# Head sums as two one-pass products of a rounded part and its remainder, and a new order of the recurrent layers' pieces

## The reference

```python
def step(s, rkvw):
    r_t, k_t, v_t, w_t = rkvw
    a = k_t[..., :, None] * v_t[..., None, :]
    out = jnp.einsum('bhi,bhij->bhj', r_t, u * a + s)
    s = a + w_t[..., :, None] * s
    return (s, out)
_, out = jax.lax.scan(step, s0, rkvw)
```

## Time and profile before

| | us |
|---|---|
| median of 3 runs (3200.41 to 3202.28) | 3200.64 |
| the profiled execution's own time | 3201.94 |
| its span (first to last instruction) | 3200.2 |
| busy: TensorE / VectorE / ScalarE | 3063.3 / 2338.7 / 1808.8 |
| recurrent steps end, attention starts, about | 2300 |

### The profile page before, as it was taken

The page is one execution under the profiler, slowest core; times in us unless marked ns, Lnnn a source line. Parts: engine busy times, 40 slices in busy tenths (PEclk is TensorE's granted clock), DMA queues, the critical chain, the costliest instruction groups (busy, mean ns, idle before and its releaser), DMA issues.

```text
span 3200.2 us, 77104 instructions
## 1 busy us (share of the span) xinstructions
PE 3063.3 (96%) x32684; PEld 2287.3 (71%) x32684; DVE 2338.7 (73%) x3819; ACT 1808.8 (57%) x3311; POOL 226.9 (7%) x457
## 2 busy tenths in 40 slices
PE   6899999999999999999999999997998998998998
PEld 4667777777777777777777777775665665665666
DVE  3788788887888787887887788876377566566566
ACT  3556555565655555555556555555366556556555
POOL 0000000000000000000000000000110101111010
PEclk8889999999999999999999999998999999999999
DMA  3223333343333333344333333343334224234131
GB/s 132 65 89 126 126 107 127 108 153 132 126 126 126 126 105 129 108 148 137 126 119 133 122 104 129 107 174 116 106 80 108 56 66 108 65 84 104 41 80 41
DMA packets 110357, 349.41 MB, mean 109 GB/s; under 512 B 22848, under 2 KB 56256, under 8 KB 84032
## 3 DMA queue, kind: packets, MB, share of 16 engines
q0 software_dynamic: 39936, 234.91, 23.2%
q1 hardware_dynamic: 69648, 106.28, 10.5%
q10 hardware_dynamic: 432, 3.28, 0.3%
HBM read 252.11 MB, written 16.78 MB: 84 GB/s over the span
## 4 chain that ended last, share of the span: by engine, by line
PE 87%; DVE 7%; ACT 4%; issue 1%; DMA 1%; SPq 0%; ACTq 0%; DVEq 0%
PE psum L734 42%; PE psum L743 6%; PE psum L901 5%; PE psum L919 4%; PE psum L871 3%; PE psum L800 3%; PE psum L861 3%; PE psum L784 3%; PE psum L891 3%; DVE psum L1727 2%; PE psum L876 2%; PE psum L687 2%; PE psum L699 2%; PE psum L867 1%; PE psum L667 1%; DVE mem L1732 1%
## 5 line engine op out<-in xcount | busy, mean ns | idle before, releaser
L734 PE MATMUL psum<-rw 128*128 128x256 f32 x6144 | 1402.8, 384 | 9.0 <-DVE rw L1529 5.4
L734 PEld LDWEIGHTS psum<-rw 128*128 128x128 f32 x6144 | 1155.1, 191 | 218.9 <-issue 54.0
L1727 DVE CUSTOM_DVE_ANT_0 psum<-psum,mem 128x1024 f32<-128x1024 f32 x256 | 313.6, 1225 | 77.3 <-PE psum L891 77.2
L1271 ACT ACTIVATE rest<-psum,mem 128x1024 f32<-128x1024 f32 x256 | 285.1, 1114 | 89.5 <-DVE mem L1727 87.8
L1523 DVE SCALAR_TENSOR_TENSOR rw<-psum,rw 128x256 f32<-128x256 f32 x480 | 196.0, 475 | 144.8 <-PE psum L700 79.5
L1183 ACT ACTIVATE rw<-psum,own 128x256 f32<-128x256 f32 x384 | 214.5, 714 | 123.7 <-PE psum L784 123.5
L901 PE MATMUL psum<-ident,rest 128*128 128x128 f32 x2048 | 270.4, 275 | 2.7 <-DVE mem L1686 1.6
L1624 DVE TENSOR_TENSOR_SCAN rw<-rw 128x2112 f32<-128x2112 f32 x48 | 217.4, 4529 | 70.6 <-ACT rw L1176 69.1
L901 PEld LDWEIGHTS psum<-ident,rest 128*128 128x128 f32 x2048 | 235.2, 141 | 42.3 <-issue 14.7
L1919 POOL DMA_DIRECT2D rw<-big_dram x192 | 101.7, 531 | 2157.2 <-PE psum L734 2124.3
L1264 ACT ACTIVATE mem<-psum 128x512 f32<-128x512 f32 x256 | 152.1, 595 | 141.0 <-PE psum L901 141.0
(11 more groups left out here) (157 smaller groups left out, 4297.4 us busy)
## 6 DMA issues: line engine op xcount, KB each, us to landing
rw<-big_dram POOLq DMA_DIRECT2D x192, 1024.0 KB, 5.6
side<-mem POOLq DMA_DIRECT2D x256, 128.0 KB, 4.1
rw<-xs_dram SPq DMA_DIRECT2D x32, 512.0 KB, 3.8
side<-mem SPq DMA_DIRECT2D x256, 64.0 KB, 2.0
rw<-rw SPq DMA_DIRECT2D x192, 64.0 KB, 2.0
rw<-rw SPq DMA_DIRECT2D x384, 32.0 KB
xs_dram<-rw SPq DMA_DIRECT2D x24, 512.0 KB, 6.4
rw<-x_dram SPq DMA_DIRECT2D x16, 512.0 KB, 5.0
```

What stands on the lines that cost most here:

```text
L734: last = mm(t[:, o * TC:(o + 1) * TC], big[:, k, P * m:P * m + P], src[:, k, 0:TC], start=k == 0, stop=k == KT - 1, skip_group_check=True)
L1271: s_ring.empty(f(probs[:, n % HPT, :].rearrange("p (a s) -> p a s", a=2), s_ring.bank(n, "s"), ACT.Exp, scale=-1.0, bias=mx[:, n % 8:n % 8 ...
L1727: maxima.inc(nc.vector.tensor_tensor_reduce(t, t, mbias.rearrange("p (a s) -> p a s", a=2), 1.0, 3.4e38, ALU.add, ALU.min, accum_out=mx[:, ...
```

## The change

Each factor tile is parted in two. ScalarE writes it rounded to float32r (`rounded`), VectorE writes factor minus rounded, again as float32r (`remainder`), and TensorE adds two float32r products with a float32r copy of `blk` in one PSUM tile. That is one more ScalarE and one more VectorE instruction for each of the nine tiles of a unit. The two parts have two buffers each (`high`, `low`), taken in turn: a rounding waits until TensorE is done with the tile two before. The factors themselves now lie in the mixtures' slots (`factors`). `blk` lies where `own_t0` is later, `add4` is dropped for `pick4`.

```diff
-    def sum_heads(it, name, src):
-        t = opened(b_ring, it, name)
-        b_ring.fill(mm(t, blk, src, start=True, stop=True), it, name)
...
+    def products(it, name):
+        if (it, name) == (0, "P0a"):
+            pe.wait_ge(blk_rounded, 1)
+        pe.wait_ge(low_dve.sem, low_dve.at(it, name))
+        n = SUMS.index(name) % 2
         t = opened(b_ring, it, name)
+        mm(t, blk_r[:].bitcast(F32R), high[n].bitcast(F32R), start=True, stop=False)
+        b_ring.fill(mm(t, blk_r[:].bitcast(F32R), low[n].bitcast(F32R), start=False, stop=True), it, name)
...
+    def rounded(it, name):
+        act.wait_ge(leaf.sem, leaf.at(it, name.lower()))
+        n = SUMS.index(name)
+        if n >= 2:
+            act.wait_ge(b_ring.full, b_ring.full_at(it, SUMS[n - 2]))
+        elif it:
+            act.wait_ge(b_ring.full, b_ring.full_at(it - 1, SUMS[-1]))
+        high_act.inc(f(high[n % 2].bitcast(F32R), factors(it, name), ACT.Copy), it, name)
...
+    def remainder(it, name):
+        dve.wait_ge(high_act.sem, high_act.at(it, name))
+        n = SUMS.index(name)
+        low_dve.inc(tt(low[n % 2].bitcast(F32R), factors(it, name), high[n % 2].bitcast(F32R).bitcast(F32), ALU.subtract), it, name)
...
-B_TILES = P0a P0b P1 P2a P2b VT0 VT1 KT0 KT1 P4a P4b P4c P4d U00 ...
+B_TILES = P0a P0b P1 P2a VT0 VT1 P2b P4a P4b KT0 KT1 P4c P4d U00 ...
-C_TILES = fr0 fr1 fk0 wo0 wo1 fk1 s1 fv0 fv1 m1 s2 i1
+C_TILES = fr0 fr1 fk0 wo0 fk1 wo1 fv0 s1 fv1 m1 s2 i1
```

More of the change, by code:

```diff
@@ L111 @@
 O_TILES = [("O0", "dve"), ("O1", "dve")]
-C_TILES = [(2, "fr0", "act"), (2, "fr1", "act"), (2, "fk0", "act"), (1, "wo0", "dve"), (1, "wo1", "dve"), (2, "fk1", "act"), (1, "s1", "act"), (2, "fv0", "dve"), (2, "fv1", "dve"), (1, "m1", "dve"), (1, "s2", "act"), (1, "i1", "dve")]
+C_TILES = [(2, "fr0", "act"), (2, "fr1", "act"), (2, "fk0", "act"), (1, "wo0", "dve"), (2, "fk1", "act"), (1, "wo1", "dve"), (2, "fv0", "dve"), (1, "s1", "act"), (2, "fv1", "dve"), (1, "m1", "dve"), (1, "s2", "act"), (1, "i1", "dve")]
@@ L124 @@
 F_ACT = ["kk0", "kk1"]
-CONSTS = 12
+SUMS = ["P0a", "P0b", "P1", "P2a", "P2b", "P4a", "P4b", "P4c", "P4d"]
+HIGH_ACT = list(SUMS)
+LOW_DVE = list(SUMS)
+CONSTS = 11
 def laid_out():
     at, n = {}, 0
-    for name, size in [("blk", P), ("pick4", P), ("pars", LAYERS * PARS), ("s_first", KT * B * 32), ("s_now", KT * B * 32),
+    for name, size in [("blk_r", P), ("pick4", P), ("pars", LAYERS * PARS), ("s_first", KT * B * 32), ("s_now", KT * B * 32),
                        ("first_edges", 2 * KT * B), ("half_edges", 2 * 2 * KT * B), ("small_w", SMALL)] + [(f"slot{i}", SLOT) for i in range(NSLOT)] + [
@@ L261, in build @@
         with nc.sbuf_tensor("rw", [P, RW_COLS], F32) as rw:
+            pass
+        parts_at, parts_size = RW_AT["parts"]
+        with nc.sbuf_tensor("blk_r", [P, P], F32) as blk_r, nc.sbuf_tensor("pick4", [P, P], F32) as pick4, \
+                nc.sbuf_tensor("between", [P, parts_at - 2 * P], F32), \
+                nc.sbuf_tensor("parts", [P, parts_size], F32) as parts:
             pass
@@ L843, in batch_tile @@
                     pe.wait_ge(*d_ring.empty_at(b, f"sum{sh}"))
-                    last = mm(t, add4[:], sums(b)[:, 512 * sh:512 * sh + 512], start=True, stop=True)
+                    last = mm(t, pick4, sums(b)[:, 512 * sh:512 * sh + 512], start=True, stop=True)
                 elif name[:4] == "mean":
@@ L946, in _ @@
                     products(b, "P2a")
-                    products(b, "P2b")
-                if 0 < n and has_n:
-                    norm_a(n, "i1")
+                if s == ITS:
+                    batch_tile(0, "k01")
                 if has_c:
@@ L953, in _ @@
                     values_by_token(b)
+                    products(b, "P2b")
+                if 0 < n and has_n:
+                    norm_a(n, "i1")
+                if has_e:
+                    feed(e, "fk", 1)
+                if has_b:
+                    products(b, "P4a")
+                    products(b, "P4b")
                 if has_c:
@@ L1765, in _ @@
                 if has_e:
-                    norm_c(e, "mixk")
+                    norm_c(e, "mixr")
+                if has_b:
+                    products1(b)
+                    level1(b)
                 if has_c:
+                    gated(c, 0)
                     gated(c, 1)
                 if has_b:
-                    level1(b)
+                    remainder(b, "P0a")
+                    remainder(b, "P0b")
+                if has_e:
+                    norm_c(e, "mixk")
+                if has_b:
+                    products2(b, 0)
+                    products2(b, 1)
+                    level2(b)
+                    own_values(b)
                 if 0 < n and has_n:
@@ L1789, in _ @@
                 if has_b:
-                    level4(b)
+                    remainder(b, "P4a")
+                    remainder(b, "P4b")
+                if s == ITS:
+                    after(0, "k00")
+                if has_c:
+                    residual(c, 0)
+                if has_b:
+                    gather(b, "P2b", "o2b", 0, 2)
+                if s == ITS:
+                    after(0, "k01")
+                if has_b:
+                    values(b, "P4a", 1, 4, 0)
                 if 0 < n and has_n:
@@ L1845, in _ @@
                 if has_b:
-                    scan(b, 1)
-                    own_turned(b, 1)
+                    group_mean(b, 0)
                 if has_n:
-                    mixed(n, "r")
+                    mixed(n, "g")
                 if has_c:
```

335 lines of the change are left out of this document (167 added, 168 removed).

## The result

| | before | after |
|---|---|---|
| median of 5 runs | 3200.72 us (3200.41 to 3202.28) | 3219.74 us (3212.38 to 3229.21) |
| profiled execution, its span | 3201.94, 3200.2 us | 3215.64, 3213.9 us |
| granted clock | 0.986 | 0.975 |
| first scan to first scan, mean of 21 steps | 90.08 us | 90.55 us |

The ratio is 1.0058 (95% interval 1.0037 to 1.0078). The forecast was 3123 us with a range of 3104 to 3162 and a chance of 0.04 for slower: it was wrong by 97 us and in its sign.

The account below looks back on a forecast made before the run. It took TensorE's list to bound the recurrent steps: 3.81 + 0.34 - 0.3 (handoffs) - 0.3 (DMA) = 3.55 us a step, times 22 is 78 us, from 3201.94, less 1.3 to the median: 3123 us, range 3104 to 3162.

Parts of the forecast that it names:

- which makes TensorE's list 90.03 - 4.15 = 85.9 us: TensorE's work in one steady step, summed from durations, falls by 4.15 us to 85.9 us.
- Products, 4.54 us: A step's nine head sums on TensorE, as float32r product pairs, take 4.54 us instead of 8.35, saving 3.81.
- Rival 4: Float32r products of the head sums run at the float32 pace, so nothing is saved there: 3206 us, chance 0.04.
- its 0.34 us go as well: TensorE's wait ahead of P4a for ScalarE to empty a bank disappears, since P4a moves ahead of the keys' transposes: 0.34 us.
- VectorE's chain, 86.2 us: The circle through VectorE's longest stretch and TensorE's list keeps a step from being shorter than 86.2 us, handoffs included.
- rival 1: VectorE's chain becomes the bound, its short operations holding the engine longer: step 87.7 us, 3150 us, chance 0.19.
- 0.3 for all handoffs: Small waits between TensorE's list and VectorE's chain cost 0.3 us a step, between 0 and 1.5.
- DMA, 0.3 us a step: The third group of updates waits 0.3 us a step for the copies of v_m, bounds 0 and 2.8.
- rival 2: The copies of v_m land late, a wait of 2.3 us a step instead of 0.3: 3167 us, chance 0.10.
- The turn of the buffers: Rounding waits for TensorE's tile two before, remainder for rounding, TensorE for remainder: some 1.6 us a turn.
- rival 3: The turn of the two buffers shows on TensorE and costs 4.7 us a step, slower than before: 3213 us, chance 0.05.
- 22 steps, nothing in the first and last: The saving counts in 22 TensorE-bound steps; the first and last unit's steps gain 0 each, bounds -3 and +4 us.

Follow-up runs that it names:

- a_r0: The changed kernel with r's first half projection back between the two halves of the state's outputs on TensorE; 3172.27 us, ratio 0.9914.
- c7: The changed kernel with s2 between k's halves, r's first half ahead of i1, third updates later, the second norm's reciprocal earlier on VectorE; 3147.37 us, 0.9834.
- the two pairs of kernels: The changed kernel and c7, each against its own order with single float32 products: 3219.7 against 3295.0 us, 3147.37 against 3222.89 us.
- a_wide: The changed kernel with neighbouring 32-column output products joined into 64 columns, half as many matmuls, outputs left wrong; 3129.21 us, 0.9778.
- a_plain: The changed kernel's order alone, each head sum one float32 product again, without roundings and subtractions; 3295.01 us, ratio 1.0301.

## Why the prediction was wrong, point by point

- **"which makes TensorE's list 90.03 - 4.15 = 85.9 us"**, taken as the time that TensorE needs for a step, is the step that failed. The list was summed from durations, as if TensorE had every instruction when it wants it; the sum put the supply of instructions and the clock behind a stall at nothing. Measured are 90.55 us a step, with 2.1 us of issue waits in the outputs alone (43.8 us in 24 times). The change joined four pieces into 320 pairs, and I looked at that order for waits on other engines and on transfers, not for its density. The trace of before had the warning. In its last unit's step, where no r stands between the halves, its own timeline reads:

```profile
2201.88 2.33 PE L800 MATMUL psum<-rw 128*32 128x32 f32 x128 [6.17 <-ACT rw L1155]
2205.01 0.74 PE L800 MATMUL psum<-rw 128*32 128x32 f32 x32 [0.80 <-DVE rw L1639]
2207.20 1.80 PE L800 MATMUL psum<-rw 128*32 128x32 f32 x96 [1.45 <-issue]
```

  No rival held this mechanism either; none of the four is what happened. Price: 47.5 us by a_r0, of which 35 are issue waits and some 12 the lower clock. That is half of the 97 us by which the forecast missed: a_r0's 3172 us is still above its range. Another 25 us are between a_r0 and c7, the waits for i1 and for the copies above all; the last 24 follow below.
- **Products, 4.54 us**: 4.81 measured. Of the saving of 3.81 us 3.54 are in the chain and 3.4 in the two pairs of kernels. Right, 0.3 us too hopeful. Rival 4 (the float32 pace) is refuted by 0.23 us a product.
- **"its 0.34 us go as well"**: no. The same wait, for ScalarE to empty the values' transpose, now stands ahead of P2b (7.2 us in 21 times), the tile that the change put behind it. The wait belongs to the two banks, not to P4a.
- **VectorE's chain, 86.2 us** (rival 1): bounded, not measured. VectorE did what I counted. The 87.7 us of the rival are refuted: c7's shortest steps are 86.8 us, and six of a_wide's, with VectorE's list as it was, are 85.9 to 86.0, so the chain is no longer than about 86. The waits for VectorE are i1's, 0.5 us a step in after (9.9 us), covered when 3.65 us of projection stand ahead of it, and 0.9 us in all in the outputs. I had allowed 0.3 for all handoffs.
- **DMA, 0.3 us a step**: 11.6 us in 12 of the steps, 0.5 a step over all. Mechanism right, size a little low; rival 2 asked for over 40 us in total.
- **The turn of the buffers** (rival 3): TensorE waits for remainders 12.5 us in all, and all of it ahead of 201 us, in the first unit. Slower it was, as this rival said, but not by it.
- **22 steps, nothing in the first and last**: the gain or loss counts in the 21 steps between the scans (9.9 us of loss); the start is 1.0 us later (201.49 against 200.48) and the rest behind the last of these scans 2.8 us longer, 3213.9 - 2103.12 against 3200.2 - 2092.25. Sum 13.7, the difference of the spans.

Between c7 (3147) and the forecast (3123) are 24 us, and 13 more, since the forecast had allowed 0.6 us of waits a step: 7.5 are P2b's wait, 7.4 issue waits that stay, 6 the products' 0.27 us a step, 1.9 the copies, some 5 the 22nd step counted and the end. Some 9 us are left; they lie within TensorE's busy time, which is 86.6 us a step in c7 where before's 89.7 less the measured saving of 3.54 would be 86.2, and I can't say in which pieces.

## What to carry to other kernels

A list of durations is not the time of an engine that runs hundreds of small instructions in a row: mark every long run of small load-and-matmul pairs as a place where the supply can fail, and keep a long product between such runs. Here runs of 288 and 320 pairs cost 1.4 and 2.1 us a step in issue waits, runs of up to 160 or 192 pairs 0.1 to 0.6. When a change has two parts, price them apart; here a gain of 75 us was hidden behind a loss of 94, and one piece moved back turned slower into faster. And where before has one irregular step (its first or last), read it: it shows what the regular ones hide.

## What the runs showed of the hardware that I had not expected

- TensorE's instructions come in blocks of 256, and in a dense run the next block is there 3.5 us after the last (1043.00 to 1046.57), while 128 pairs of 32 columns are used up in 2.3 us. The packet that brings a block took 0.9 to 1.7 us in transfer at the 26 stalls of after, and TensorE went on 1.1 to 1.6 us after it had landed.
- Behind 1.7 us of such a stall TensorE ran at half its clock for some 3 us (0.73, 0.50, 0.92 in the windows), though it had work.
- 64 small matmuls on two of four partition groups take nearly as long as 128 on all four (2.15 and 2.35 us).
- A float32 product is four instructions (two loads, two matmuls): 64 of them moved the stream by 256, and the split of a head sum into two float32r products left their number unchanged. That is why after and a_plain stall at the same places (75 left at 1137.48 in the one and at 1163.56 in the other).
